# A graph layer on one core: block 0 of the edges sorted by scatters of single records, and attention on two pairs of node tiles in a step

## What is computed

```python
# graph attention over edges, per source node
Wh = xn @ W_w + W_b
e = leaky_relu(Wh[dst] @ a_w[:256] + Wh[src] @ a_w[256:] + a_b[0], 0.2)
att = segment_softmax(e, src)
gnn = relu(segment_sum(att[:, None] * Wh[dst], src))
# linear attention over all nodes, 8 heads; q and k pass elu(.) + 1
mix = (q @ (k^T v)) / (q @ sum(k)) @ Wproj^T + bproj
x = x + gnn + mix
# mixture of experts, 8 experts, the best 2 of each node
x = x + moe(layernorm(x))        # gelu(t @ w1[e] + b1[e]) @ w2[e] + b2[e]
```

## Time and profile before

| | us |
|---|---|
| median of 3 runs | 2222.33 |
| range of the runs | 2213.17 to 2228.12 |
| span of the profiled execution | 2207.5 |
| busy: PE | 1718.1 (78%) |
| busy: DVE | 1669.8 (76%) |
| busy: ACT | 976.2 (44%) |
| busy: POOL | 994.8 (45%) |
| of POOL: 904 gathers (L664) | 921.0 |
| of PE: 1568 matmuls of the permutation (L999) | 176.9 |

### The profile page before, as it was taken

How to read it: one execution, slowest core, us unless ns; L and a number is a source line. 1 busy time by engine, 2 the same in 40 slices (tenths; PEclk the granted TensorE clock), 3 DMA queues, 4 the chain that set the end, 5 groups by cost and what they waited for, 6 DMA issues and landing times.

```text
span 2207.5 us, 40303 instructions
## 1 busy us (share of the span) xinstructions
PE 1718.1 (78%) x13588; PEld 1259.6 (57%) x13588; DVE 1669.8 (76%) x4220; ACT 976.2 (44%) x2300; POOL 994.8 (45%) x988
## 2 busy tenths in 40 slices
PE   3778785574785688888757888887888888889998
PEld 2557573463674466666535555555555555566666
DVE  5998998663566677776767887888888888886665
ACT  6322221121332233222235656666666656575655
POOL 3000003425566655655666666666666666640000
PEclk7898997796898788888968999999999999999999
DMA  5011111124554444333333333333333333860000
GB/s 174 16 59 52 51 66 32 42 84 115 145 165 130 118 120 119 102 94 90 90 90 87 86 90 83 94 83 94 82 95 92 86 92 83 89 56 11 11 20 13
DMA packets 121460, 182.21 MB, mean 83 GB/s; under 512 B 21490, under 2 KB 91902, under 8 KB 121214
## 3 DMA queue, kind: packets, MB, share of 16 engines
q0 software_dynamic: 45312, 120.06, 23.3%
q1 hardware_dynamic: 75904, 59.25, 8.6%
HBM read 152.43 MB, written 26.63 MB: 81 GB/s over the span
## 4 chain that ended last, share of the span: by engine, by line
DVE 42%; PE 23%; issue 16%; another core or an unknown queue 10%; ACT 4%; DVEq 2%; POOL 1%; DMA 0%; SPq 0%; ACTq 0%; POOLq 0%
PE bank L1255 6%; PE bank L1271 5%; DVE mloc L1615 4%; DVE big L1518 4%; DVE scr L1637 3%; DVE big L1523 3%; DVE work L1809 3%; DVE big L1520 2%; DVE big L1525 2%; DVE big L1796 2%; DVE scr L1483 2%; DVE work L1593 2%; DVE work L1610 2%; PE bank L947 1%
## 5 line engine op out<-in xcount | busy, mean ns | idle before, releaser
L664 POOL DMA_INDIRECT work<-table,tiles x904 | 921.0, 1019 | 546.6 <-PE bank L1142 277.8
L1271 PE MATMUL bank<-big 128*128 128x256 f16 x2352 | 327.7, 278 | 34.8 <-issue 34.5
L1255 PE MATMUL bank<-scr,big 128*128 128x512 f16 (+1 forms) x1248 | 282.3, 377 | 0.3 <-ACT big L871 0.3
L1140 PE MATMUL bank<-work,scr 128*128 128x257 f16 x904 | 269.9, 299 | 13.0 <-issue 10.5
L1271 PEld LDWEIGHTS bank<-big 128*128 128x128 f16 x2352 | 232.3, 99 | 78.3 <-issue 46.0
L1141 PE MATMUL bank<-work,scr 128*128 128x256 f16 x904 | 270.8, 300 | 5.9 <-issue 5.6
L1142 PE MATMUL bank<-work,scr 128*128 128x257 f16 x904 | 268.9, 297 | 5.9 <-issue 5.9
L1637 DVE SCALAR_TENSOR_TENSOR scr<-scr,gg,bank 128x257 f32<-128x257 f32 x452 | 216.7, 479 | 29.7 <-remote 16.6
L999 PE MATMUL bank<-big 128*128 128x208 f16 x1568 | 176.9, 269 | 67.7 <-DVE big L1525 60.9
L799 ACT ACTIVATE work<-bank 128x1024 f16<-128x1024 f16 x113 | 115.5, 1022 | 242.7 <-DVE mloc L1615 144.0
L999 PEld LDWEIGHTS bank<-big 128*128 128x128 f16 x1568 | 150.7, 102 | 94.6 <-issue 88.9
(11 more groups left out here) (340 smaller groups left out, 3494.1 us busy)
## 6 DMA issues: line engine op xcount, KB each, us to landing
work<-table,tiles POOLq DMA_INDIRECT x904
scr<-normed_cols SPq DMA_DIRECT2D x98, 128.0 KB
table<-big SPq DMA_DIRECT2D x49, 129.0 KB, 2.1
normed_rows<-scr SPq DMA_DIRECT2D x49, 128.5 KB, 2.6
big<-normed_rows SPq DMA_DIRECT2D x49, 128.5 KB
normed_cols<-big SPq DMA_DIRECT2D x49, 128.0 KB, 1.7
xs<-in_x_dram SPq DMA_DIRECT2D x4, 1536.0 KB, 14.2
out_dram<-work SPq DMA_DIRECT2D x48, 128.0 KB
```

Source lines behind the costliest of these rows:

```text
L664: pool.indirect_dma_start(G[:, r, j, :], None, table, bass.IndirectOffsetOnAxis(ap=col[:, t:t + 1], axis=0)).then_inc(rows_in[r // GS], 16)
L1140: pe.matmul(of[:, 0:D + 1], hi, Gh[:, r, j, 0:D + 1], start=(j == 0), stop=False)
L1255: mm = pe.matmul(bank[5 + f][:, 0:n * P], w1p[pw][:, e, h, f * P:(f + 1) * P], x2p[b % 2][px][:, h, 0:n * P], start=(h + m == 0), stop=(h ...
L1271: mm = pe.matmul(of, hTp[ph][:, k % 2, f, (j + c) * P:(j + c + 1) * P], w2p[pw][:, e, f, :], start=False, stop=(f == 1 and m == 2))
```

## The change

Block 0 is no longer permuted. Its ranks are worked out as before; DVE then computes the place of each record as one index (`ind0`), and POOL writes the 200 columns with 200 indirect DMAs, 128 records of 4 bytes each, to `sorted0` in DRAM, which SP has zeroed; POOL reads that back as block 0's `recs`. Between columns 8, 64 and 136 POOL also moves the rows for the ranks of blocks 1 to 3, which it did one after the other. 73 permutation steps are left, and the node work is spread over steps 5 to 60 of them. The one-hots of block 2 are made before block 1's ranks, not during them.

Attention takes two pairs a step: 13 units at steps 14 to 26, with second buffers for `ev`, `rv`, `qd` and four for `q_`, one reciprocal and one turn for both pairs, and the denominators in bank 7. By the formula above `F_AT` becomes 35, 43, ..., 131 and the last step 140.

```diff
-    BATCH = [0]
-    for a, z in COLS:
+    assert EREST >= COLS[0][1]
+    BATCH = [0, 0]
+    for a, z in COLS[1:]:
         BATCH.append(BATCH[-1] + (z - a) // NC)
...
+    sorted0 = nc.dram_tensor("sorted0", [P * TT, 2], F16).ap()
...
-        rec = piece(2 * H)
+        rec = piece(4 * H)
...
+        ev, rv, qd, q_ = [ev], [rv], [qd], list(q_)
+        spare = wkvT.rearrange("p h c -> p (h c)")
+        for n, of in enumerate((ev, rv)):
+            of.append(spare[:, n * 2 * D:(n + 1) * 2 * D].rearrange("p (h n) -> p h n", h=2))
+        qd.append(wwx.rearrange("p h c -> p (h c)")[:, 0:2 * D].rearrange("p (h n) -> p h n", h=2))
+        q_ += [v.rearrange("p j c -> p (j c)")[:, 0:2 * D].rearrange("p (h n) -> p h n", h=2) for v in x_rows]
...
-        NB0 = 10
-        NODE_AT = {NB0 + w * (BATCH[-1] - 1 - NB0) // (W - 1): w for w in range(W)}
+        NB0 = 5
+        NODE_AT = {NB0 + w * (BATCH[-1] - 13 - NB0) // (W - 1): w for w in range(W)}
         assert len(NODE_AT) == W and max(NODE_AT) < BATCH[-1]
         BASES_AT = 4
-        assert BATCH[1] > NB0 > BASES_AT
+        FIRST_COLUMNS = COLS[0][1]
+        ROWS_AFTER = (0, 8, 64, 136)
...
-        A_AT = {A_FROM + p: p for p in range(PW)}
+        QW = -(-PW // 2)
+        A_AT = {A_FROM + u: u for u in range(QW)}
+
+        def pairs_of(u):
+            return range(2 * u, min(2 * u + 2, PW))
...
+            sp.dma_start(sorted0.rearrange("(p t) c -> p (t c)", p=P), tiles[:, 0:TT].bitcast(F16)).then_inc(blank, 16)
...
-                if s + 1 in A_AT:
-                    p = A_AT[s + 1]
+                for p in pairs_of(A_AT[s + 1]) if s + 1 in A_AT else ():
...
-            for b, (a, z) in enumerate(COLS):
+            def rank_rows(b):
+                a, z = COLS[b]
                 n = (z - a) // 2
                 pool.wait_ge(s_v, b + 1)
...
+            rank_rows(0)
+            pool.wait_ge(blank, 32)
+            pool.wait_ge(s_ind, 1)
+            for c in range(FIRST_COLUMNS):
+                if c in ROWS_AFTER[1:]:
+                    rank_rows(ROWS_AFTER.index(c))
+                pool.indirect_dma_start(sorted0, bass.IndirectOffsetOnAxis(ap=ind0[:, c:c + 1], axis=0),
+                                        recs0[:, c, :], None).then_inc(scattered, 16)
+            pool.wait_ge(scattered, 16 * FIRST_COLUMNS)
+            pool.dma_start(recs[:, 0, :, :].rearrange("p t c -> p (t c)"),
+                           sorted0.rearrange("(p t) c -> p (t c)", p=P)).then_inc(scattered, 16)
             for b in range(NBL):
                 pool.wait_ge(s_dest, b + 1)
-                pool.wait_ge(s_rec, b + 1)
+                if b:
+                    pool.wait_ge(s_rec, b)
+                else:
+                    pool.wait_ge(scattered, 16 * (FIRST_COLUMNS + 1))
...
+                if p > 1:
+                    act.wait_ge(a_qT, p - 1)
                 else:
                     act.wait_ge(k_kk, PW)
+                    act.wait_ge(c_psum, 1)
                 of = bank[5][:, :].rearrange("p (h n) -> p h n", h=2)[:, :, 0:n]
-                act.activation(ev[:, :, 0:n], of, ACT.Exp)
-                act.activation(rv[:, :, 0:n], of, ACT.Relu).then_inc(a_raw, 1)
-
-            def reciprocals_sb(p):
-                n = of_pair[p] * P
-                act.wait_ge(a_rt, p + 1)
-                if p:
-                    act.wait_ge(a_ex, p)
-                act.copy(recT[:, 0:n], bank[1][0:H, P:P + n]).then_inc(a_rsb, 1)
+                act.activation(ev[p % 2][:, :, 0:n], of, ACT.Exp)
+                act.activation(rv[p % 2][:, :, 0:n], of, ACT.Relu).then_inc(a_raw, 1)
...
-                if s in A_AT:
-                    queries_raw(A_AT[s])
+                for p in pairs_of(A_AT[s]) if s in A_AT else ():
+                    queries_raw(p)
...
+            column_ranks(0)
+            column_sums(1)
+            column_bases(1)
+            for b in range(1, NBL):
...
-            def denominators(p):
-                pe.wait_ge(a_qT, p + 1)
+            def denominators(u):
+                pe.wait_ge(a_qT, pairs_of(u)[-1] + 1)
                 pe.wait_ge(c_ksum, 1)
-                if p:
-                    pe.wait_ge(a_rsb, p)
-                for j in range(of_pair[p]):
-                    for h in range(2):
-                        mm = pe.matmul(bank[1][:, j * H:(j + 1) * H], q_[p % 2][:, h, j * P:(j + 1) * P],
-                                       sums_k[:, h, :], start=(h == 0), stop=(h == 1))
+                if u:
+                    pe.wait_ge(a_rec, u)
+                    pe.wait_ge(a_x, pairs_of(u - 1)[0])
+                for p in pairs_of(u):
+                    for j in range(of_pair[p]):
+                        at_ = (p % 2 * 2 + j) * H
+                        for h in range(2):
+                            mm = pe.matmul(bank[7][:, at_:at_ + H], q_[p % 4][:, h, j * P:(j + 1) * P],
+                                           sums_k[:, h, :], start=(h == 0), stop=(h == 1))
                 mm.then_inc(a_den, 1)
...
+            def reciprocals_turned(u):
+                pe.wait_ge(a_rec, u + 1)
+                if u:
+                    pe.wait_ge(a_rsb, u)
...
+                if p // 2 + 1 < QW:
+                    pe.wait_ge(a_rec, p // 2 + 2)
...
-                    expanded(A_AT[s - 3])
+                    expanded(2 * A_AT[s - 3])
...
+                for p in pairs_of(A_AT[s])[0:1] if s in A_AT else ():
+                    queries(p)
...
+                for p in pairs_of(A_AT[s - 3])[1:] if s - 3 in A_AT else ():
+                    expanded(p)
...
-                if s in A_AT:
-                    queries(A_AT[s])
                 if s - 3 in A_AT:
-                    projected(A_AT[s - 3])
+                    projected(2 * A_AT[s - 3])
+                for p in pairs_of(A_AT[s])[1:] if s in A_AT else ():
+                    queries(p)
+                for p in pairs_of(A_AT[s - 3])[1:] if s - 3 in A_AT else ():
+                    projected(p)
...
-                    if b + 1 < NBL:
+                    if b != 1 and b + 1 < NBL:
                         one_hots(b + 1, k_ * W // len(chunks_b), (k_ + 1) * W // len(chunks_b))
+                    elif b == 1:
+                        pass
...
+                if b == 0:
+                    for k, of in enumerate((v1h, v2h)):
+                        dve.tensor_copy(recs0[:, :, k], of[:, a:z])
+                    link(dve.tensor_scalar(si[:, 0:m], si[:, 0:m], (P * CH).bit_length() - 1, None, ALU.arith_shift_right))
+                    link(dve.scalar_tensor_tensor(srank[:, 0:m], si[:, 0:m], float(CH), bi[:, 0:m], ALU.mult, ALU.add))
+                    dve.scalar_tensor_tensor(ind0, ai[:, 0:m], float(TT), srank[:, 0:m], ALU.mult, ALU.add).then_inc(s_ind, 1)
+                    one_hots(2)
+                    column_counts(1)
+                    bases(1)
+                    continue
...
-                if s - 4 in A_AT:
-                    mixed(A_AT[s - 4])
+                for p in pairs_of(A_AT[s - 4])[1:] if s - 4 in A_AT else ():
+                    mixed(p)
+                if s - 2 in A_AT:
+                    reciprocals(A_AT[s - 2])
                 if s - 3 in A_AT:
-                    divided(A_AT[s - 3])
+                    divided(2 * A_AT[s - 3])
+                for p in pairs_of(A_AT[s - 1])[0:1] if s - 1 in A_AT else ():
+                    queries_one(p)
...
-                if s - 2 in A_AT:
-                    reciprocals(A_AT[s - 2])
-                if s - 1 in A_AT:
-                    queries_one(A_AT[s - 1])
+                for p in pairs_of(A_AT[s - 3])[1:] if s - 3 in A_AT else ():
+                    divided(p)
+                for p in pairs_of(A_AT[s - 1])[1:] if s - 1 in A_AT else ():
+                    queries_one(p)
...
+                if s - 3 in A_AT:
+                    mixed(2 * A_AT[s - 3])
```

More of the change, by code:

```diff
@@ L430, in graph_layer @@
             at_ += X
+        assert F_AT[0] > B2_AT + 1
         UP_AT = {F_AT[b] + e: (b, e) for b in range(NBAT) for e in range(X)}
@@ L737, in _ @@
             turned_norm(0)
-            for b in range(NBL):
+            for b in range(1, NBL):
                 for n in range(BATCH[b], BATCH[b + 1]):
@@ L1665, in queries_one, with reciprocals @@
                 dve.wait_ge(a_raw, p + 1)
[L1666 to L1668 removed]
+                if p > 3:
+                    dve.wait_ge(a_qd, p - 3)
+                dve.scalar_tensor_tensor(q_[p % 4][:, :, 0:n], ev[p % 2][:, :, 0:n], 1.0, rv[p % 2][:, :, 0:n], ALU.min, ALU.add
                                          ).then_inc(a_qT, 1)
[L1671 to L1674 removed]
+            def reciprocals(u):
+                n = sum(of_pair[p] for p in pairs_of(u)) * H
+                dve.wait_ge(a_den, u + 1)
+                dve.reciprocal(rec[:, 0:n], bank[7][:, 0:n]).then_inc(a_rec, 1)
             def contexts(n):
```

54 lines of the change are left out of this document (25 added, 29 removed).

## The result

The changed kernel takes 2386.05 us (median of 4, 2377.0 to 2390.2) where the kernel before takes 2223.3 us (2213.2 to 2228.1): ratio 1.075, 95% interval 1.072 to 1.079. It is 7.5% slower; the forecast was 2125 us.

What follows compares the result with a forecast made beforehand. DVE mostly bounds sorting, a chain across engines the loop. 2207.5 us, less 38 (attention in double steps) and 60 (block 0 sorted by scatters), gives 2109.5; the runs' median stands 14.8 higher, so 2125 us, range 2070 to 2200.

Steps and rivals of the forecast that it cites:

- part 2: Sorting stage: block 0 sorted by POOL scatters instead of DVE permutation steps, priced at -60 us.
- costed at nothing: Attention: new waits on bank 7 and a_rec, and SP's second pair of loads per step, priced at zero.
- 8 us of node work: Later blocks' permutation: 8 us added because 49 pieces of node work fall into 56 steps instead of 88.
- Long POOL streams hold up PE: Sorting rival: unbroken indirect transfers cause the unnamed waits; 103 to 146 us added, total 2207 to 2250 us; chance 0.15.
- 16 scatters and ranks with no such wait: Argument against the POOL-stream rival: 364.8 to 384.8 us of the earlier trace shows scatters beside ranks without unnamed waits.
- In the loop POOL issues eight at a time without it: Argument against the POOL-stream rival: the edge loop's transfers, issued eight at a time, show no such hold-up.
- The double step: Attention stage: a loop step with two pairs takes 16.8 us, against 13.45 us for a single step.
- The chain: Attention step: dependent work passing between PE, ACT and DVE, lengthened by second-pair work, sets the step time: 16.85 us.
- the matmuls between, eight a pair and about 0.7 us: Double attention step: denominator matmuls between DVE's second-pair addition and its reciprocals, adding about 0.7 us.
- The first set of queries: Double attention step: one set of PE queries, 1.90 us, lies while PE waits for DVE.
- the tail: FFN-only steps at the end: 12 fewer at 6.18 us each, -74.1 us.
- The lock of the Trainium skill: Sorting rival: DVE locks POOL out, one scatter per 2.88 us permutation step; +41 us, total 2225 us; chance 0.04.

Runs made afterwards that it cites:

- e_both2_p10: Changed kernel with reordered attention step, plus 10 short POOL iotas after each 8 scatters of block 0: 2230.5 us, ratio 0.995 to the kernel before.
- short set: Experiment runs sharing a chip, in which the unedited kernel before takes 2009 us.
- e_attn: Kernel before with only the attention part of the change, sorting as before: 2035.2 us, ratio 1.014; run again as e_attn_b: 2248.2 us, ratio 1.004.
- e_attn2: Kernel before with only the attention part, PE's first queries moved ahead of denominators and DVE's reciprocals later: 2208.6 us, ratio 0.995.
- e_sort: Kernel before with only the sorting part of the change, attention in single steps as before: 1962.5 us, ratio 0.977.
- e_both2: Changed kernel with the reordered attention step, no pauses among the scatters: 2353.9 us, ratio 1.058 to the kernel before.
- long sets: Experiment runs, each set sharing a chip, in which the kernel before takes 2218 to 2240 us.
- e_iota: Kernel before, sorting and attention untouched, with 200 added iotas on POOL and no added scatters: 2010.9 us in one run.

## Why the prediction was wrong

**The step that failed** is a term that the sum of part 2 lacks: what the new stream costs PE, and DVE that waits for PE. It isn't even among those "costed at nothing". Part 2 priced what the scatters cost POOL, and what is behind POOL, and left PE's pace untouched but for 8 us of node work. In the surroundings of the first measurement the stream costs the loop's start 668.1 - 521.7 = +146 us where -60 was forecast; 206 of the 261 us between forecast and result.

**The rival had it, at a chance of 0.15, and too small.** "Long POOL streams hold up PE" named the unnamed waits of the earlier trace rows and the stream as their common place. Both arguments against it were of a kind that couldn't tell. "16 scatters and ranks with no such wait" is 20 us of stream; in the changed kernel the first stream starts at 67 and PE is held from about 100. "In the loop POOL issues eight at a time without it" is a stream with pauses, and e_both2_p10 shows that 2.8 us per 8 are enough. Its price of 103 to 146 us took a share of 0.4 to 0.57 from streams of 32 and 39 transfers and multiplied; but PE's distances grow from 0.70 to 2.8 us within a stream, DVE is released up to 17.9 us late on top, POOL then waits 121.4 us for the engines that it has held, and the stage stretches.

**The double step** was taken at 16.8 us and measured 18.95, 17.95 in the short set. The chain was the right one, and the wait on bank 7 had been named; the term that was mis-sized is "the matmuls between, eight a pair and about 0.7 us". In the double step of e_attn shown above they are 3.55 us, at a granted clock of 0.50 and behind a PE that stood 1.33 us, and DVE waits 3.81 us for them. The first set of queries, which was to lie "while PE waits for DVE", took 3.2 us and made DVE wait 2.41 us. e_attn2 moved these two; its double step is 2.6 us shorter than that of e_attn_b. ("ACT's wait for PE" of 74.2 us was an inference: the earlier trace rows says "remote", no engine.) Of the 52 us by which the forecast of steps 14 to 47 is short, the double steps are 13 x 2.15 = 28. The eight steps behind them are 8 x (14.27 - 11.94) = 19: they now hold the end of the last double unit and the preparation of the second bias, which lay in attention steps before, and DVE is busy 76 of 114 us in them. That this is the cause is read from the schedule; no run moves those parts alone. The last 5 us are the twelve steps after that (13.23 against 12.83).

```profile
1130.00:1244.00 114.00, 71.21 (x502) 51.05 (x501) 76.10 (x194) 26.85 (x79) 64.33 (x65) 0.71 0.28 75
```

**Right**, by their own numbers: the tail, -72.4 us against -74.1; all batches moved by 12 steps; scatters 1.41 us apart in e_sort, where DVE permutes beside them (56 in 82.6 to 160.4 us), and 1.29 in the changed kernel, where it mostly waits (56 in 83.3 to 154.2 us), against 1.28 to 1.5; and, where the stream doesn't hold PE, the whole of part 2: 101.7, 430.5 and 445.2 us against 98, 432 and 448. There the part gained 46 us and not 60, as the kernel before begins its loop at 501 too and not at 522.

**The lock of the Trainium skill** (SBUF - State Buffer, "SBUF: two separate sides") was a rival at 0.04. The traces agree in sign only: a scatter to sorted0 is busy 1122 ns on the mean in e_sort, where DVE works beside it, and 1027 ns in the changed kernel, where DVE mostly waits (the two are from different sets), and in neither do the scatters stand 2.88 us apart. The victim of the stream was PE, which by that section waits for no one at SBUF's ports; no run here shows by which path it is held.

```profile
L660 POOL DMA_INDIRECT sorted<-scr x200 | 224.4, 1122 | 88.9 <-issue 60.7 <-DVE scr L1534 28.3
```

```profile
L670 POOL DMA_INDIRECT sorted<-scr x200 | 205.4, 1027 | 88.9 <-issue 60.6 <-DVE scr L1558 28.3
```

**What stays open**: by which path an indexed transfer of POOL holds back PE's instructions and the releases behind them, and what makes a set long or short. The sorting part by itself was run in a short set alone. The plain transfers, at 0.54 us each, made streams of 30 to 40 us, and the scatters begin to hold PE only 10 to 40 us into a stream, so they aren't quite acquitted.

## What to carry to other kernels

Waits that the trace can't name are evidence: ask in which stretch they all lie and what runs unbroken there, and give a mechanism that explains them its full chance before you lengthen that stretch. Work moved to an "idle" engine is not free if it makes that engine's stream unbroken; price it by a kernel of before with the same stream added and nobody reading it, and try a short pause every few instructions. And measure a change of a few per cent in more than one set of runs: the same sorting part was 2.3% faster in one set, and about 6% slower in others (e_both2 over e_attn2, 1.058/0.995).

## What the runs showed of the hardware

- In the first measurement and in the three long sets that had one, an unbroken stream of POOL's indexed transfers (about 1.3 us each) slowed PE's instructions to one in 0.70 us, then 1.4, 2.1 and 2.8, from 10 to 40 us into the stream until up to 7 us behind it. DVE and ACT didn't start in such steps, but DVE was released as much as 17.9 us behind PE's last matmul. In short sets the same streams did nothing of the kind (98 sums in 4.5 us). 16 or 128 indices made no difference, iotas (46.7 of 57 us) none, and a pause of 2.8 us in every 13 nearly ended it.
- The same kernel took 2009 us in two sets and 2218 to 2240 in four, on one and the same chip in both ways. With the longer time goes that PE waits for "issue" in the loop, where POOL gathers in bursts. In 1200 to 1700 us the FFN's second matmuls wait so in the first trace of the kernel before:

```profile
PE bank L1271 <- issue: 22.4, 33, 1.2
```

and in the short set the same matmuls (L1285 of e_iota) have no such wait among all that the view lists; a step with edges and FFN takes 11.7 us there, 12.83 in the earlier trace rows.
